# A clamp as a pairwise maximum, the mask product behind the key transposes, gelu products ahead of square sums, and the queries first on ACT behind the gated rounds

## The reference

```python
def attn_layer(x, Wqkv, qs, ksc, Wo):        # 16 heads of 64, windows of 32 tokens
    q, k, v = split(x @ Wqkv)
    q = l2norm(q) * qs;  k = l2norm(k) * ksc  # norm floored at 1e-12
    q, k = rotary(q), rotary(k)
    sim = q @ k.T * 8.0                       # each window sees itself and the one before
    sim = where(mask, -max, sim)
    return softmax(sim) @ v @ Wo

def ffn_layer(x, g, bln, W1, b1, W2, b2):     # inner width 341
    a, gate = split((layernorm(x) * g + bln) @ W1 + b1)
    return a * gelu(gate) @ W2 + b2

for i in range(6):
    x = attn_layer(shift_tokens(x), ...) + x
    x = ffn_layer(shift_tokens(x), ...) + x
```

## Time and profile before

| | us |
|---|---|
| median of 3 runs | 3688.31 |
| lowest and highest run | 3687.0, 3690.43 |
| the profiled execution | 3693.28 |
| its span, first to last instruction | 3691.5 |
| PE busy | 3335.8 (90%) |
| DVE busy | 2987.8 (81%) |
| POOL busy | 2604.2 (71%) |
| ACT busy | 2192.6 (59%) |
| mean granted TensorE clock | 0.986 of full speed |

### The profile page before, as it was taken

One profiled execution on the slowest core, in us unless ns is written; L12 is line 12 of the kernel. 1 busy time (PEld: TensorE's weight loads), 2 busy tenths in 40 slices (PEclk: granted clock), 3 DMA queues, 4 the chain that ended last, 5 costly groups with the idle time before them and its releaser, 6 DMA issues.

```text
span 3691.5 us, 149928 instructions
## 1 busy us (share of the span) xinstructions
PE 3335.8 (90%) x63806; PEld 2687.6 (73%) x63806; DVE 2987.8 (81%) x4403; ACT 2192.6 (59%) x4154; POOL 2604.2 (71%) x2893
## 2 busy tenths in 40 slices
PE   6999999999999999999779899999999999999997
PEld 4777777777777777777667777777777777777775
DVE  5888888888888888888558888888888888888874
ACT  4665666666666665666436656666666666666664
POOL 5877776777677777777348677767776777777763
PEclk8999999999999999999979999999999999999998
DMA  2211211221221221121112112112212212211111
GB/s 79 68 49 52 65 49 49 59 58 44 61 58 47 57 59 50 55 57 48 28 29 67 51 51 64 50 50 58 58 44 61 58 47 61 56 50 46 50 38 38
DMA packets 117856, 195.41 MB, mean 53 GB/s; under 512 B 23756, under 2 KB 36552, under 8 KB 117192
## 3 DMA queue, kind: packets, MB, share of 16 engines
q1 hardware_dynamic: 117192, 185.82, 18.5%
HBM read 33.71 MB, written 1.05 MB: 9 GB/s over the span
## 4 chain that ended last, share of the span: by engine, by line
PE 52%; DVE 15%; issue 15%; ACT 12%; POOL 6%; DVEq 0%; ACTq 0%; POOLq 0%
PE o_ps L939 7%; PE tr L954 7%; PE s_ps L910 5%; PE tr L923 5%; DVE ss_raw L708 4%; ACT qt L543 4%; PE f_ps L1000 4%; DVE rotated L701 3%; POOL prob L425 3%; PE qk_ps L853 3%; ACT sq L527 3%; PE qk_ps L855 3%; PE qk_ps L854 3%; PE tr L880 3%; DVE row_max L715 2%
## 5 line engine op out<-in xcount | busy, mean ns | idle before, releaser
L419 POOL TENSOR_TENSOR rotated<-rotated 128x1024 f32<-128x1024 f32 x384 | 914.9, 2383 | 23.0 <-DVE rotated L701 23.0
L425 POOL TENSOR_TENSOR prob<-prob,rden 128x512 f32<-128x512 f32 x384 | 434.6, 1132 | 630.1 <-DVE rden L733 630.1
L448 POOL TENSOR_TENSOR rotated<-rotated,rn 128x1024 f32<-128x1024 f32 x384 | 730.8, 1903 | 30.3 <-POOL rn L440 0.2
L695 DVE TENSOR_TENSOR rotated<-qk_ps,rot 128x1024 f32<-128x1024 f32 x384 | 468.4, 1220 | 326.2 <-ACT sq L527 325.7
L543 ACT ACTIVATE qt<-tr 128x512 f32<-128x512 f32 x384 | 229.7, 598 | 441.4 <-PE tr L880 441.4
L701 DVE TENSOR_TENSOR rotated<-qk_ps,rot 128x512 f32<-128x512 f32 x768 | 490.7, 680 | 0.0
L711 DVE TENSOR_SCALAR ss<-ss_raw 128x16 f32<-128x16 f32 x384 | 468.4, 1220 | 13.3
L708 DVE TENSOR_REDUCE ss_raw<-sq 128x16 f32<-128x1024 f32 x384 | 463.9, 1208 | 0.0
L567 ACT ACTIVATE pt<-tr 128x512 f32<-128x512 f32 x384 | 229.5, 598 | 330.8 <-PE tr L923 330.8
L910 PEld LDWEIGHTS s_ps<-kt,qt 64*32 64x32 f32 x24576 | 359.5, 107 | 87.1 <-issue 87.1
L910 PE MATMUL s_ps<-kt,qt 64*32 64x64 f32 x24576 | 421.5, 218 | 0.0
(11 more groups left out here) (150 smaller groups left out, 7222.2 us busy)
## 6 DMA issues: line engine op xcount, KB each, us to landing
vs<-vn SPq DMA_DIRECT2D x384, 192.0 KB
vs<-vtail SPq DMA_DIRECT2D x384, 64.0 KB, 2.4
vtail<-vn SPq DMA_DIRECT2D x384, 64.0 KB, 2.2
staging<-layer_wqkv_dram SPq DMA_DIRECT2D x72, 256.0 KB, 3.5
wo<-layer_wo_dram SPq DMA_DIRECT2D x12, 512.0 KB, 4.5
xs<-xa SPq DMA_DIRECT2D x48, 128.0 KB, 2.3
fs<-xa SPq DMA_DIRECT2D x48, 128.0 KB, 2.5
xs<-xa SPq DMA_DIRECT2D x48, 127.8 KB, 2.4
```

The lines of the kernel that those rows point to most:

```text
L419: nc.gpsimd.tensor_tensor(rot_c[h], rot_c[h], rot_s[h], ALU.add).then_inc(rot_added, 1)
L425: nc.gpsimd.tensor_tensor(prob[h][:, :, :], prob[h][:, :, :], rden[h][:, :].unsqueeze(2).to_broadcast([P, 2 * PAIRS, KEYS]), ALU.mult).the ...
L448: nc.gpsimd.tensor_tensor(folded, folded, rn[:, :].unsqueeze(2).to_broadcast([P, 2 * UH, DH]), ALU.mult).then_inc(qkn_ready, 1)
L695: nc.vector.tensor_tensor(rot_c[h], src, part(0, 0, DH), ALU.mult)
```

## The change

It has five parts. (1) The clamp (L711) becomes a reduction by maximum over pairs: the sums are written to every other element of `ss_floor`, whose other elements hold the floor from a memset at the start, and the upper limit is dropped. (2) The mask matmul leaves `scores` and is issued between `key_heads` and `project_v`, with its wait for the differences of the unit before. (3) On DVE the six products `hidden` move from the start of slot 9 to slot 8, between `differences` and `square_sums`. (4) On ACT `queries` and `keys` stand first in the slot behind the gates, ahead of `outputs` and `exps`. (5) On PE `down` moves from the end of its slot to the place between `scores` and `prob_major`.

```diff
--- before.py
+++ after.py
@@ -33,7 +33,6 @@
 QK_SCALE = 8.0
 SQUARE_SCALE = 256.0
 SQUARE_FLOOR = 1e-24 * SQUARE_SCALE ** 2
-SQUARE_CEIL = 2.0 ** 64
 EPS = 1e-5
 MASKED = -1e30
 ONE, DMA_ONE = 1, 16
@@ -116,7 +115,7 @@
         mac_fd = [rotated[:, s, 0, :, :].rearrange("p h d -> p (h d)") for s in range(SEQS)]
         mac_sq = [rotated[:, s, 1, :, :].rearrange("p h d -> p (h d)") for s in range(SEQS)]
         ss = [sb(f"ss{h}", [P, 2 * UH]) for h in range(2)]
-        ss_raw = sb("ss_raw", [P, 2 * UH])
+        ss_floor = sb("ss_floor", [P, 2 * UH, 2])
         ss_log = sb("ss_log", [P, 2 * UH])
         guess = [sb(f"guess{h}", [P, 2 * UH]) for h in range(2)]
         three = sb("three", [P, 2 * UH])
@@ -384,6 +383,7 @@
                 nc.gpsimd.memset(vtail[h][:, :, :], 0.0).then_inc(zeros_ready, 1)
                 nc.gpsimd.memset(kt[h][:, :, :], 0.0).then_inc(zeros_ready, 1)
             nc.gpsimd.memset(three[:, :], 3.0)
+            nc.gpsimd.memset(ss_floor[:, :, :], SQUARE_FLOOR)
             nc.gpsimd.memset(mean_mat[:, :], 1.0 / P).then_inc(zeros_ready, 1)
             nc.gpsimd.memset(minus_half[:, :], -0.5).then_inc(zeros_ready, 1)
             nc.gpsimd.memset(xs[:, 0:1], 0.0).then_inc(zeros_ready, 1)
@@ -605,11 +605,15 @@
                 act.wait_ge(zeros_ready, 8)
                 tokens_high(p * SEQS * DEPTH)
                 for n in slots(p):
+                    after_gated = ffn_of(p, n - 1, GATED_AT) is not None
+                    if live(p, n) and after_gated:
+                        queries(n)
+                        keys(n)
                     if live(p, n - 2):
                         outputs(n - 2)
                     if live(p, n - 1):
                         exps(n - 1)
-                    if live(p, n):
+                    if live(p, n) and not after_gated:
                         queries(n)
                         keys(n)
                     if live(p, n + 2):
@@ -705,10 +709,10 @@
                 h = U % 2
                 dve.wait_ge(sq_ready, ONE + U + 1)
                 dve.wait_ge(ss_ready, ONE + U)
-                nc.vector.tensor_reduce(ss_raw[:, :], sq[:, :, :], AX_X, ALU.add).then_inc(summed, 1)
+                nc.vector.tensor_reduce(ss_floor[:, :, 0], sq[:, :, :], AX_X, ALU.add).then_inc(summed, 1)
                 dve.wait_ge(summed, ONE + U + 1)
                 dve.wait_ge(rn_ready, ONE + max(0, U - 1))
-                nc.vector.tensor_scalar(ss[h][:, :], ss_raw[:, :], SQUARE_FLOOR, SQUARE_CEIL, ALU.max, ALU.min).then_inc(ss_ready, 1)
+                nc.vector.tensor_reduce(ss[h][:, :], ss_floor[:, :, :], AX_X, ALU.max).then_inc(ss_ready, 1)
 
             def row_maxima(U):
                 dve.wait_ge(s_ready, ONE + U + 1)
@@ -775,8 +779,6 @@
                 macaron_ln(2 * p * SEQS)
                 tokens_low(p * SEQS * DEPTH)
                 for n in slots(p):
-                    if (it := ffn_of(p, n, GATED_AT + 1)) is not None:
-                        hidden(it)
                     if live(p, n - 1):
                         prob_sums(n - 1)
                     if (it := staged_for(p, n, 2)) is not None:
@@ -796,6 +798,8 @@
                     if live(p, n):
                         row_maxima(n)
                         differences(n)
+                    if (it := ffn_of(p, n, GATED_AT)) is not None:
+                        hidden(it)
                     if live(p, n + 2):
                         square_sums(n + 2)
 
@@ -894,11 +898,14 @@
                                                rot_c[h][:, 1, 2 * a:2 * a + 2, :].rearrange("p h d -> p (h d)"), ident[:, :])
                 last.then_inc(ktp_ready, 1)
 
+            def mask_scores(U):
+                pe.wait_ge(dif_ready, ONE + U)
+                nc.tensor.matmul(s_ps[:, :], ident16[:, :],
+                                 mask[:, min(U // 2 % TPS, 1), :].unsqueeze(1).to_broadcast([P, PAIRS, 2 * KEYS]),
+                                 start=True, stop=False, skip_group_check=True)
+
             def scores(U):
                 h, t = U % 2, U // 2 % TPS
-                pe.wait_ge(dif_ready, ONE + U)
-                nc.tensor.matmul(s_ps[:, :], ident16[:, :], mask[:, min(t, 1), :].unsqueeze(1).to_broadcast([P, PAIRS, 2 * KEYS]),
-                                 start=True, stop=False, skip_group_check=True)
                 pe.wait_ge(kt_ready, ONE + U + 1)
                 for a in range(PAIRS):
                     for gg in range(2):
@@ -1012,8 +1019,11 @@
                     if live(p, n):
                         query_heads(p, n)
                         key_heads(p, n)
+                        mask_scores(n)
                         project_v(n)
                         scores(n)
+                    if (it := ffn_of(p, n, DOWN_AT)) is not None:
+                        down(it)
                     if live(p, n - 1):
                         prob_major(p, n - 1)
                     if live(p, n - 2):
@@ -1026,8 +1036,6 @@
                         variances(it)
                     if (it := ffn_of(p, n, SPREAD_AT)) is not None:
                         spread(it)
-                    if (it := ffn_of(p, n, DOWN_AT)) is not None:
-                        down(it)
                     if (it := ffn_of(p, n, GATED_AT)) is not None:
                         gated(p, n, it)
                 if p == 0:
```

## The result

| | before | after |
|---|---|---|
| median, us | 3688.43 (3687.0 to 3690.43) | 3489.76 (3487.24 to 3491.3) |
| profiled span, us | 3691.5 | 3488.1 |

The changed kernel takes 0.946 of the time of the kernel before (95% interval 0.9444 to 0.9477), 198.7 us less. The prediction was 3445 us in a range from 3405 to 3520: the direction and the range held, and the saving was 44 us smaller than the 243 forecast.

What follows compares the result with a forecast made beforehand. The prediction took time to be PE's own work plus PE's gaps, PE being busy 90% of the span. Its terms, 28 + 123 + 50 + 42 = 243 us, gave a median of 3445 us, range 3405 to 3520.

Steps and rivals of the forecast that it cites:

- clamp, through the waits for the probabilities: L711 on DVE: the maximum takes 0.18 us, so POOL's product starts sooner; 0.29 us in 98 waits, 28 us saved.
- mask product: PE, ahead of the values: fills their gap, so scores follow the values at once; 384 × 0.32 = 123 us saved.
- gelu products: DVE, ahead of the square sums: frees `f_ps` before PE's fourth gated round; 1.14 × 44 = 50 us saved.
- queries first, `down` early: Slot behind the gates: query copy starts 0.95 us sooner, `down` covers the later exponentials; 0.95 × 44 = 42 us saved.
- the 0.32 us fit: Gap before the values on PE: assumed longer than its recorded 0.25 us, so it holds the mask product's whole 0.32 us.
- The interplay: Waits for POOL's probabilities: PE arriving 0.32 us sooner in each of two slots cuts the clamp's 0.93 us to 0.29.
- the output additions come later by `down`: Slot behind the gates: additions are delayed by `down`, but stand just as close to the slot's end in plain slots.
- The collision: Rival: L755 waits under POOL's L419, then precedes POOL's product, 0.70 us later; 36 times, 25 us, 3470 us; chance 0.19.
- the prediction's own signs of being wrong: PE waiting before the mask product, L755 or L680 beyond 1 us, a wait behind `down`, or plain slots near 7.4.
- POOL's keeping up: Rival: POOL keeps up fully, PE's earlier arrival counted once at the waits for probabilities; 3413 us; chance 0.14.
- A clamp no shorter: Rival: L711's replacement is no faster, its part brings nothing and 98 waits grow by 0.64 us; 3536 us; chance 0.06.
- a wait at the mask product: Rival: PE's in-order queue waits there for late differences in each of 384 slots; 3829 us at 1 us; chance 0.03.

Runs made afterwards that it cites:

- the single edit: One group of edits made alone in the kernel before: gelu products first 3642.3 us (0.9863); queries first with `down` early 3658.54 us (0.9906).
- the elementwise maximum: Changed kernel with the clamp as an elementwise maximum of two SBUF tiles instead of the pairwise reduction: 3568.55 us, 0.9675.
- the run without the collision: Changed kernel with the normed tokens kept in PSUM, so their low part (L759) has one SBUF input instead of two: 3471.93 us, 0.9411.
- the work on POOL, in the right order: Changed kernel with weight splits, rotary tables and the variance's root moved between `scale_probs` and `inverse_norms`: 3442.72 us, 0.9332.

## Why the prediction was right, and where not

The single terms, read in the trace of the changed kernel:

| part | forecast, us | in the trace, us | from |
|---|---|---|---|
| clamp, through the waits for the probabilities | 28 | 37 | 93.2 − 56.0 |
| mask product | 123 | 81 | 384 × (7.49 − 7.28); 74 by the medians, 7.46 − 7.27 |
| gelu products | 50 | 50 | the 44 gaps are gone; the single edit's span gives 51 |
| queries first, `down` early | 42 | 35 | the single edit's span |
| sum | 243 | 203 | spans: 203.4 |

The direction, the range and the mechanism held, and one term was mis-sized, the mask product. That these terms meet the spans to the microsecond is luck, since the mask product alone is known to 7 us. The errors also had both signs, 42 and 7 us too much and 9 too little.

**The clamp.** That the 1.22 us are POOL's lock, that the maximum takes 0.18 us and that DVE saves nearly 400 us (397 at the clamp; 356 in DVE's busy time, of which L759 took back 28) were right, and the elementwise maximum shows the cause. That DVE's lateness reached the end through the waits for the probabilities was right too. The point missed is that it also made the gap before the fourth gated round. In the sum this does no harm, since the gap was counted once, under the gelu products. Whoever asked which edit brings what would have been told 28 us for one that brings 107 alone and, against the form that is blocked (the elementwise maximum), 79 within the change.

**The mask product.** This is the step that failed: "the 0.32 us fit", and with it 384 × 0.32 = 123. They did fit in front of the values, which start at the same moment. But the 0.32 us from the mask product to the scores held about 0.1 of a pause that belongs to the scores, and that stayed behind the values. What could be moved was 0.24. By the medians the scores come 0.23 us sooner, and 0.03 of that is lost again behind them: 0.20 to 0.21 came out. So the lower bound of 0.23 (88 us) was missed as well, by 7 us or more, and its reason, that no more than the recorded gap can be filled, was not what set the size. What lies between two starts is the first product's own time plus a pause ahead of the second, and only the former can be moved. The 42 us missing here are nearly all of the 44 by which the time was off.

**The interplay** that the prediction charged to the clamp (0.32 us in two slots for each wait) is real: PE's earlier arrival comes back as waiting for POOL, 125 instead of 93 us with the mask alone, 56 instead of 27 with the clamp. With the true 0.21 the same working gives (0.93 − 0.42) × 98 = 50 us, against 37. It fits the waits that it was read from: the 31 behind one weight split should shrink by 0.93 − 0.42 and, for the collision, 0.06 less, that is by 0.45, and the one shown went from 1.18 to 0.71. It is wrong for others of the 98. 22 were of about 0.5 us and could give no more. And 11, behind two weight splits (L398 and L403), were no fault of DVE's: the clamp alone leaves them at 0.4 us each (4.4 us), and PE's earlier arrival makes them 0.8 (9.2 us).

**The gelu products** came out as worked, with the gap gone in all 44 rounds.

**Queries first, and `down`.** In the slot behind the gates the working held. PE's rows there, in the changed kernel:

```profile
743.55 0.39 PE L857 MATMUL qk_ps<-wqkv_hi,xs_hi 128*128 128x512 f32 x1
...
746.23 0.50 PE L857 MATMUL tr<-wqkv_hi,xs_hi 128*128 128x512 f32 x1
```

The values start 2.68 us into the slot; before it was 3.64 (the slot of the earlier trace rows begins at 1079.34), so they come 0.96 us sooner, for 0.95 foretold. The slot as a whole lasts 9.78 us (743.55 to 753.33) instead of 10.62, and there is no wait for the probabilities behind `down`. The step that it lacked is the end of a pass: `down` stands ahead of the last output projection, which has nothing behind it to hide in, and costs 5.6 us (the two last distances between table loads, 27.0 and 27.4 us instead of 24.3 and 24.5) to 7 us (the run that puts it back). The prediction had written that the output additions come later by `down` and took it as free, which holds for plain slots alone.

**The rivals.** The collision came as described, L759 at 1.6 us in 31 rounds, each behind a weight split, for 36 foretold; L684 (L680 before), with two SBUF inputs as well, stayed at 637 to 684 ns, and POOL's product beside it takes 1.38 us in both kernels. So one of the prediction's own signs of being wrong appeared, an instruction beyond 1 us in many rounds, but its price was wrong too. POOL's product does not start 0.70 us later; it starts as POOL's addition ends, and takes 1.50 us instead of the 1.44 that it had beside L755 before. That is 0.06 us a round, 2 us in all, for 25 foretold. The 18 us of the run without the collision include what the kernel before paid already. The plain slot, at 7.27, came out between the forecast's 7.17 and the 7.4 that it named as a sign of being wrong. POOL's keeping up did not happen: waits of 0.7 us where it has extra work. A clamp no shorter, and a wait at the mask product, are ruled out: the profile has no wait for the differences at L903.

## What to carry to other kernels

A tiny instruction with a long record is waiting for something; compare its end with the ends of the other engines' instructions, and try a form that does not need what is shared. Before a distance between two starts is counted as the price of the first instruction, look whether the second would keep a pause behind any other neighbour. Savings on one engine that each remove the same gap do not add, and an engine that arrives sooner waits longer for the next one: here the work on POOL, in the right order, was worth another 47 us.

## What the runs showed of the hardware

An elementwise maximum of 128x16 elements with two SBUF inputs took between 174 and 2274 ns beside POOL's work, one with scalar bounds between 174 and 2426, a reduction of 128x32 between 185 and 190. A blocked one ended 28 to 42 ns behind the end of the POOL instruction that it overlapped. An instruction of 128x512 with two SBUF inputs that arrived during POOL's addition took 1600 ns instead of 700; it went ahead of POOL's next instruction, though that was ready, and that one took 1.50 instead of 1.04 us (1.44 where the DVE instruction had started 0.16 us before it). With one of the inputs in PSUM neither happened. The 64x32 score products started 0.32 us behind an fp32 product of 512 columns that is otherwise followed after 0.24, 0.32 behind a bf16 one of 512 columns and 0.13 behind one of 64: a pause of nearly 0.1 us ahead of them in each case, if the bf16 products cost by column what the fp32 ones do (an estimate).
